# Four modulation rows: columns and a trip through memory in place of full-precision row products

## The reference

```python
mod = (_silu(L0_c) @ L0_wmod).reshape(L0_c.shape[0], 6, 1, -1)
sa, ca, ga, sb, cb, gb = (mod[:, 0], mod[:, 1], mod[:, 2], mod[:, 3], mod[:, 4], mod[:, 5])
ga = (2 * (ga >= 0) - 1) * jnp.maximum(jnp.abs(ga), 0.25)
gb = (2 * (gb >= 0) - 1) * jnp.maximum(jnp.abs(gb), 0.25)
h = _layernorm(x, axis=-1) * (1 + ca) + sa
x = x + ga * _L0_attn_ref(h, L0_attn_Wq, L0_attn_Wk, L0_attn_Wv, L0_attn_Wu, L0_attn_Wo)
h = _layernorm(x, axis=-1) * (1 + cb) + sb
x = x + gb * _L0_ffn_ref(h, L0_ffn_weight, L0_ffn_bias)
```

## Time and profile before

| | |
|---|---|
| median of 3 runs | 508.58 us (508.37 to 510.7) |
| the profiled execution | 510.15 us |
| its span on the slowest core, core 0 | 508.1 us |
| spans of the other cores | 499.9 to 504.5 us |
| TensorE matmuls busy on core 0 | 405.4 us, 80% of the span |
| VectorE busy | 299.4 us, 59% |
| ScalarE busy | 237.8 us, 47% |
| moved by DMA | 84.92 MB, 167 GB/s on average |

### The profile page before, as it was taken

One profiled execution on the slowest core, in us unless ns is written; L12 is line 12 of the kernel. 1 busy time (PEld: TensorE's weight loads), 2 busy tenths in 40 slices (PEclk: granted clock), 3 DMA queues, 4 the chain that ended last, 5 costly groups with the idle time before them and its releaser, 6 DMA issues.

```text
span 508.1 us, 6419 instructions; the slowest of 8 cores (499.9 to 508.1 us)
## 1 busy us (share of the span) xinstructions
PE 405.4 (80%) x2028; PEld 189.4 (37%) x2068; DVE 299.4 (59%) x524; ACT 237.8 (47%) x348; POOL 57.7 (11%) x90
## 2 busy tenths in 40 slices
PE   0004568968989999787796989998999989998984
PEld 0002234424544444433442434443444434444441
DVE  0388550184867627446886456663666637665884
ACT  1134165454457323156756385445764367643431
POOL 1021011020000000000002111111201212011321
PEclk9999996999999999999898899998999989999998
DMA  7999969999956665920229950656335752455686
GB/s 189 336 335 192 268 189 234 215 195 265 304 221 195 248 221 183 306 92 1 83 70 301 318 140 10 124 118 119 54 77 90 159 85 55 111 84 124 88 142 143
DMA packets 17984, 84.92 MB, mean 167 GB/s; under 512 B 2336, under 2 KB 2336, under 8 KB 12832
## 3 DMA queue, kind: packets, MB, share of 16 engines
q0 software_dynamic: 7776, 32.51, 33.8%
q1 hardware_dynamic: 10176, 52.01, 31.4%
HBM read 68.26 MB, written 24.64 MB: 183 GB/s over the span
## 4 chain that ended last, share of the span: by engine, by line
PE 51%; DVE 19%; ACT 12%; issue 11%; DMA 4%; POOL 1%; DVEq 1%; SPq 1%; ACTq 0%; POOLq 0%
PE pb L315 43%; DVE junk L454 4%; DVE bn L266 3%; DMA wa<-wmod_a 3%; ACT rn L619 2%; PE pb L380 2%; ACT osq L609 2%; DVE h L705 2%; DMA stage<-wmod_b 1%; DVE am L708 1%; PE pb L617 1%; PE pb L343 1%; ACT xq L719 1%; DVE wm_c L424 1%; ACT rn L622 1%
## 5 line engine op out<-in xcount | busy, mean ns | idle before, releaser
L315 PE MATMUL pb<-wk_s,h 128*128 128x512 bf16 x249 | 62.0, 405 | 9.1 <-DVE h L463 5.8
L315 PE MATMUL pb<-fq,xqT 128*128 128x512 bf16 x247 | 60.5, 385 | 3.4 <-ACT xqT L731 2.2
L315 PE MATMUL pb<-wo_s,u_s 128*128 128x512 bf16 x254 | 61.2, 394 | 1.5 <-DVE u_s L599 1.4
L315 PE MATMUL pb<-h,wu_s 128*128 128x512 bf16 x248 | 60.5, 385 | 0.3
L315 PE MATMUL pb<-h,wq_s 128*128 128x512 bf16 x250 | 60.2, 384 | 0.2
L315 PE MATMUL pb<-wv_s,h 128*128 128x512 bf16 x249 | 59.3, 386 | 0.4
L285 PE MATMUL pb<-id_b,xh 128*128 128x128 bf16 x128 | 13.3, 260 | 49.5 <-ACT xh L275 47.9
L624 DVE SCALAR_TENSOR_TENSOR q_s<-rn,pb 128x512 bf16<-128x512 f32 x32 | 22.0, 687 | 44.6 <-ACT rn L622 42.1
L315 PEld LDWEIGHTS pb<-wk_s,h 128*128 128x128 bf16 x256 | 25.9, 103 | 43.2 <-issue 18.4
L371 DVE SCALAR_TENSOR_TENSOR accb<-stage,silc,accb 128x1024 f32<-128x1024 f32 x28 | 36.0, 1285 | 8.9 <-DMA stage<-wmod_b 6.5
L315 PEld LDWEIGHTS pb<-wo_s,u_s 128*128 128x128 bf16 x256 | 25.7, 101 | 33.4 <-issue 6.4
(11 more groups left out here) (92 smaller groups left out, 561.1 us busy)
## 6 DMA issues: line engine op xcount, KB each, us to landing
stage<-wmod_b SPq DMA_DIRECT2D x16, 1024.0 KB, 7.0
xr<-x_tm POOLq DMA_DIRECT2D x16, 512.0 KB, 16.6
wa<-wmod_a SPq DMA_DIRECT2D x8, 1024.0 KB, 22.2
xr<-x_tm SPq DMA_DIRECT2D x16, 512.0 KB, 3.6
out_tm<-row_gbb SPq DMA_DIRECT2D x4, 2048.0 KB, 20.1
out_tm<-xr POOLq DMA_DIRECT2D x15, 512.0 KB, 8.1
out_tm<-h POOLq DMA_DIRECT2D x15, 512.0 KB, 5.5
stage<-wo SPq DMA_DIRECT2D x4, 1024.0 KB, 14.0
```

Of the source, the lines that this page charges most:

```text
L315: t = PE.do(lambda e, dc=dc: e.matmul(pb[bank][:], lhs(dc), rhs(dc), start=(dc == 0), stop=(dc == NC - 1)), *after, each(dc) if each else ...
```

## The change

The four vectors `ga`, `sb`, `cb`, `gb` are now made as `sa` and `ca` are: `wmod_b` lies in memory feature by feature, feature 8p+k on partition p, `mod_piece` multiplies it in its stage buffer by `silr` and sums along the row into column `2c+d` of `mod_c[v]`, and `mod_fin` does the sign, maximum and 1+ steps on 128x8 columns. `put` writes the column tile (4 KB, 32 bytes for each partition) to a new tensor `rows` in memory and `get` reads that row back onto all 128 partitions (512 KB), both on the SP queue. The same is done for the bias times `gb` (`put(3)`) and for the weight's scales times `gb` (`put(4)`, in the new `last_row`). The columns `silc` and the products L380 and L815 are gone. For the weight's scales to lie in the same order, the feed-forward weight is loaded with rows 8p+ec, and `ffn_transp` writes every eighth column of `fq`. The list `mods` is in a new order: 4 pieces of vector 0, `mod_fin(0)`; 4 pieces of vector 1, `mod_fin(1)`, the four `wo_piece`; 4 pieces and `mod_fin` of vectors 2 and 3; `get(3)`. The reads `get(0)`, `get(1)`, `get(2)` stand in the SP queue right behind the load of the next vector's first piece. `wa_sum` writes into `wa` itself and no longer into one `junk` tile.

```diff
-                in1=accb[:], op0=ALU.mult, op1=ALU.add), st_tok[n], t_acc[0])
+            st_free[n] = col_tok[v] = DVE.do(lambda e, d=d: e.scalar_tensor_tensor(
+                out=s[:, D * d:D * d + D], in0=s[:, D * d:D * d + D], scalar=1.0, in1=silr[:],
+                op0=ALU.mult, op1=ALU.mult, accum_out=mod_c[v][:, 2 * c + d:2 * c + d + 1]),
+                st_tok[n], t_silr)
+
+    def put(k, col, *after):
+
+        put_tok[k] = SP.dma(sl_p[k], bass.AP(d_rows, k * D, [[NC, 128], [1, NC]]), col[:], *after)
+
+    def get(k, row, *after):
+
+        row_tok[k] = SP.dma(sl_g[k], row[:], bass.AP(d_rows, k * D, [[0, 128], [1, D]]),
+                            put_tok[k], *after)
...
-    def mod_row(v, hf):
-
-        sl = slice(512 * hf, 512 * hf + 512)
-        t = PE.do(lambda e: e.matmul(pb[7][:], on_f[:], accb[:, sl], start=True, stop=True),
-                  t_acc[0], t_ones, b7[0])
...
+    def mod_fin(v):
...
+        col_tok[v] = t
+        put(v, gbb_c if v == 3 else m, t)
...
-            out=fq[:, :, 128 * ec:128 * ec + 128],
+            out=fq[:, :, ec::NC],
...
-        t = None
         for col, k in ((ca_c, 0), (sa_c, 1)):
             t = DVE.do(lambda e, col=col, k=k: e.scalar_tensor_tensor(
-                out=junk[:], in0=wa[dc][:, D * k:D * k + D], scalar=1.0, in1=silr[:],
-                op0=ALU.mult, op1=ALU.mult, accum_out=col[:, dc:dc + 1]), wa_tok[dc], t_silr, t,
-                wa_free.get(dc - 1))
+                out=wa[dc][:, D * k:D * k + D], in0=wa[dc][:, D * k:D * k + D], scalar=1.0, in1=silr[:],
+                op0=ALU.mult, op1=ALU.mult, accum_out=col[:, dc:dc + 1]), wa_tok[dc], t_silr)
...
+    def piece_after(v, k):
+        mod_piece(v, 0)
+        get(k, ROWS[k])
+
+    mods = [lambda c=c: mod_piece(0, c) for c in range(4)]
+    mods.append(lambda: mod_fin(0))
+    for v in (1, 2, 3):
+        mods.append(lambda v=v: piece_after(v, v - 1))
+        mods += [lambda v=v, c=c: mod_piece(v, c) for c in range(1, 4)]
+        mods.append(lambda v=v: mod_fin(v))
+        if v == 1:
+            mods += [lambda c=c: wo_piece(c) for c in range(4)]
+    mods.append(lambda: get(3, row_gbb))
...
     def last_row():
-        t = t_dg[0]
-        for hf in range(2):
...
+
+        t = DVE.do(lambda e: e.tensor_tensor(out=gws_c[:], in0=ws_c[:], in1=mod_c[3][:], op=ALU.mult),
+                   fw_tok[NC - 1], col_tok[3])
+        put(4, gws_c, t)
+        get(4, row_g, fold_tok[0])
...
-    last_rows()
+    last_row()
     fill()
```

More of the change, by code:

```diff
@@ L88, in build_nc @@
     d_wb = dram("wmod_b", [128, 4, NC, D])
+    d_rows = dram("rows", [5, D], kind="Internal")
     d_idb = dram("ident_bf", [128, 128], BF16)
@@ L141, in build_nc @@
     blk = sb("blk", [128, 128], BF16)
-    on_f = sb("on_f", [128, 128])
-    c_col = sb("c_s", [128, NC])
-    silc = sb("silc", [128, NC])
+    bias_c = sb("bias_c", [128, NC])
+    mod_c = [sb(f"mod_c{v}", [128, NC]) for v in range(4)]
+    sgn_c = sb("sgn_c", [128, NC])
+    abs_c = sb("abs_c", [128, NC])
+    gws_c = sb("gws_c", [128, NC])
+    gbb_c = sb("gbb_c", [128, NC])
     sa_c = sb("sa_c", [128, NC])
@@ L197, in build_nc @@
     sl_c = Slot(nc, "const")
-    sl_k = Slot(nc, "const2")
     sl_r = Slot(nc, "crow")
-    sl_b = Slot(nc, "bias")
+    sl_p = [Slot(nc, f"put{k}") for k in range(5)]
+    sl_g = [Slot(nc, f"get{k}") for k in range(5)]
     x_tok = {}
@@ L230, in load_stage @@
         return n
-    t_c = SP.dma(sl_c, c_col[:], d_c.ap())
     t_cr = SP.dma(sl_r, silr[:], bass.AP(d_cr, 0, [[0, 128], [1, D]]))
-    SP.dma(sl_k, id_b[:], d_idb.ap())
-    SP.dma(sl_k, id_h[:], d_idh.ap())
-    t_const = SP.dma(sl_k, blk[:], d_blk.ap())
+    SP.dma(sl_c, id_b[:], d_idb.ap())
+    SP.dma(sl_c, id_h[:], d_idh.ap())
+    SP.dma(sl_c, blk[:], d_blk.ap())
+    t_const = SP.dma(sl_c, bias_c[:], d_fb.ap())
     wa_tok = [SP.dma(sl_a[dc], wa[dc][:],
                      bass.AP(d_wa, dc * 2 * D, [[NC * 2 * D, 128], [1, 2048]])) for dc in range(NC)]
-    t_ones = DVE.do(lambda e: e.memset(on_f[:], 1.0))
     t_half = DVE.do(lambda e: e.memset(halfc, HALF))
@@ L352, in build_nc @@
     b7 = [None]
[L353 to L356, removed]
+    row_tok, col_tok = {}, {}
     fold_tok = [None]
     t_gate = [None]
+    put_tok = {}
     def mod_piece(v, c):
@@ new lines, in mod_fin @@
+    def mod_fin(v):
+        m = mod_c[v]
+        t = col_tok[v]
+        if v == 2:
+            t = DVE.do(lambda e: e.tensor_scalar_add(out=m[:], in0=m[:], scalar1=1.0), t)
+        elif v != 1:
+            t1 = DVE.do(lambda e: e.tensor_scalar(out=sgn_c[:], in0=m[:], scalar1=0.0, scalar2=2.0,
+                                                  op0=ALU.is_ge, op1=ALU.mult), t)
+            t = DVE.do(lambda e: e.scalar_tensor_tensor(out=abs_c[:], in0=sgn_c[:], scalar=1.0, in1=m[:],
+                                                        op0=ALU.subtract, op1=ALU.mult), t1)
+            t = DVE.do(lambda e: e.tensor_scalar_max(out=abs_c[:], in0=abs_c[:], scalar1=0.25), t)
+            t = DVE.do(lambda e: e.scalar_tensor_tensor(out=m[:], in0=sgn_c[:], scalar=1.0, in1=abs_c[:],
+                                                        op0=ALU.subtract, op1=ALU.mult), t)
+        if v == 3:
+            t = DVE.do(lambda e: e.tensor_tensor(out=gbb_c[:], in0=m[:], in1=bias_c[:], op=ALU.mult),
+                       t, t_const)
+        col_tok[v] = t
+        put(v, gbb_c if v == 3 else m, t)
@@ L404, in wo_piece @@
+    ROWS = {0: row_g, 1: row_sb, 2: row_cb, 3: row_gbb}
     def wo_piece(c):
@@ L698, in norm1 @@
             out=h2[g % 4][:], in0=x[:], scalar=mean[:, 0:1], in1=row_cb[:], op0=op, op1=ALU.mult),
-            row_tok[2, 1], y_out.get(g - 4), t, fw_tok[7])
+            row_tok[2], y_out.get(g - 4), t, fw_tok[7])
     def norm2(g):
@@ L856, in build_nc @@
             X[3]()
-        if g == 0:
-            last_row()
     for hf in range(2):
```

75 lines of the change are left out of this document (11 added, 64 removed).

## The result

The changed kernel is slower: 522.25 us (median of 4 executions) against 509.32 for the kernel before on the same chip, ratio 1.0227, 95% interval 1.0164 to 1.029. One of the four executions, at 530.06, ran in a slower state of the chip, with part of its cores at a lower clock; the ratios here leave such executions out, and the other three took 518.51 to 522.44. The forecast of 496.5 and its range to 505 are both missed, on the wrong side.

The account below looks back on a forecast made before the run. PE, its matmuls busy for 80% of the span and half of the chain of waits, was taken as the bound; 510.15 + 2.0 - 11.3 + 1.7 - 5.4 = 497.2, less 0.7, gave 496.5 us, range 489 to 505.

Parts of the forecast that it names:

- The strided `fq`: ACT's write of every eighth column of fq in the weight quantisation: taken as 0, bounded by 0 and +2 us.
- Vector 0, +2.0: Break in SP's loads behind put(0): xhat(12) starts later and PE passes 155.18 two us late; bounds -3.8 and +5.
- Vectors 1 to 3, -11.3: Up to 215.6 us PE waits only for the row products; removing them gains 3.0 + 2.9 + 5.4 us.
- DVE at `kv_bd`, +1.7: DVE ends its list for kv_bd at 208, against PE's arrival at 206.3; bounds 0 and +6 us.
- Weight quantisation, 0: Loads behind put(3) and get(3) land about when the feed-forward weight is read: price 0, bounds 0 to +3 us.
- `last_row`, -5.4: Row of the weight's scales: its PE and DVE work goes, gaining 5.6 us, of which DVE's q takes back 0.2.
- Behind 300 us, 0: Everything behind 300 us was taken as untouched, only shifting along: 0.
- The slower one: Rival, chance 0.07: SP's list stands still in each break, costing 10 us more than reckoned, giving 527 us.
- The doubling rival: Rival, chance 0.17: the strided write of fq doubles in price, adding 2 us to give 498.5.
- my two signs of being wrong: xhat(12) keeping PE's time would mean forecast too high; DVE waiting over 10 us at a put, too low.
- the line "L444 at 1.1 or at 2.2": Listed check on ACT's write of fq: its time in the trace would be 1.1 or 2.2 us.
- The five stretches at the head of the prediction: Time PE loses around the row products: 3.80, 3.00, 2.9, 5.40 and 5.5 us, put together as 20.7.

Follow-up runs that it names:

- the two pairs of kernels: The kernel before with only the strided write added, 535.78 us; the changed kernel with only that write made contiguous, 497.69 us.
- the first probes: The kernel before with three more instructions for each of 19 write or read forms behind its last output; executed once, no kernel time given.
- the first experiment: The changed kernel with fq written in runs of 128 and rows 3 and 4 written as 4-byte elements: 527.09 us, ratio 1.0329 to the kernel before.

## Why the prediction was wrong

**The strided `fq`: the step that failed.** The form of the argument was right. The pace of the stretch hides a slower evacuation up to a point, and what is over it counts. The size was not. I had no row, took 0, and ended the bound at a doubling. The price is 4.3 times: 4805 ns, and 5.88 for a step against a pace of 2.85. Put into my own steps, seven steps are 5.88 - 2.85 = 3.0 longer and the last evacuation 3.7: 24.9. The stretch shows 23.9, the medians of the two pairs of kernels 24.6 and 26.6. But the parts are others, so the closeness of the sum is partly luck. From the start of the first evacuation to the last transposes the kernel before takes 17.65 us (243.84 to 261.49) and the changed one 40.02 (241.23 to 281.25): 22.4. From there to the first result of `wproj` it is 4.23 and 5.81, 1.6 more, at a granted clock of 1.00 and 0.72. The last evacuation, which I had on the path, is not on it. The doubling was no bound from a row, only a factor that felt large. What could have been reckoned was the point from which it decides: the pace of 2.85 less one filling of the bank with its gaps, 0.9, leaves 2.0 us for the evacuation, 1.8 times its 1.113. Beyond that each further microsecond costs seven. With a write that no row showed and a rule of the Trainium skill against it, that belonged into the rivals as the slower case, with more than the 0.07 that I gave to SP's list.

The Trainium skill's rule (SBUF — State Buffer, "Door 1: The DMA port swizzle (why `[64,N]` ≈ `[32,N]`)", two hits in a 16-byte line for full speed) pointed the right way in its part on hits. The same note of the Trainium skill names 8 bf16 as how far one can stride for free; the step of 8 took 4783 here instead of 1113, and the measurement decides. By the two hits the runs of two at 16-byte distance are fast, which L871 agrees with (1207). By them bf16 with step 4, two hits in a line, would be fast as well; L875 of the first probes shows 2522. So the rule on hits fits the 4-byte pieces here and not the single 2-byte ones.

**Vector 0, +2.0.** PE passes its point 1.6 late, `xhat(12)` starts at 141.96 (140.6 reckoned). Right in sum, by two errors that cancel: the break is longer (put 7.1 for 2, load 9.4 for 6.0), and it begins 3.9 earlier, as vector 0's last piece landed at 115.89, not 118.83, and the column steps ended at 119.4, not 122.6. The queue was not drained as I had assumed, with the DMA engines 97% busy over the put; over the eight cores this put takes 4.2 to 7.1. The nearest row for a small write was the wrong one.

**Vectors 1 to 3, -11.3, and DVE at `kv_bd`, +1.7.** PE is through at 205.85 (206.3 reckoned). DVE starts the cast at 211.54 in the profiled execution of after, at 208.69 and 209.87 in the two kernels that differ from it only behind that point; 208 was reckoned. Against PE's 206.3 the term is 2.4 to 5.2, inside its bounds of 0 to +6, above the value taken.

**Weight quantisation, 0.** In after 1.6 are lost, with PE at half clock behind its 4.73 us wait for DVE (that the clock is the whole of it no run shows); with contiguous writes 0.4, and DVE waits 0.90 for the weight's first load. The bounds of 0 to +3 held.

**`last_row`, -5.4.** The stretch from group 0 to group 1 is 5.1 us shorter in after and 4.8 with the contiguous write. Right to within 0.6.

**Behind 300 us, 0.** Wrong by 3 to 4 us in my favour. With the contiguous write three stretches of groups are shorter by 0.9, 1.5 and 0.8, with the same work. The one from 331.74 before and its answer after:

```profile
331.74:350.73 18.99, 16.76 (x78) 7.44 (x78) 10.27 (x16) 11.37 (x17) 3.34 (x4) 0.94 0.57 109
```

```profile
348.34:366.46 18.12, 16.16 (x82) 7.32 (x80) 10.28 (x15) 11.37 (x17) 3.62 (x4) 1.00 0.56 112
```

The granted clock is 0.94 in the one and 1.00 in the other, and likewise 0.91 and 1.00 in the stretch that is 1.5 shorter. I had no step for it. What makes the clock fall there in the kernel before, no run here takes apart. So that the contiguous version came out at 497.69 beside 496.5 is partly luck: it gained 6.0 until `wproj` where 7.6 was reckoned, 4.8 in `last_row`, and 3.5 that I hadn't counted.

**The rivals.** The slower one named SP's list as its mechanism. In the changed kernel that isn't what happened, but the first experiment shows that it was a real danger: with 4-byte elements the same put holds the list 15.8 and 20.7 us and costs 29.4 (527.09 against 497.69; 29.6 by the ratios). The doubling rival had the place and the direction, not the price. Neither of my two signs of being wrong came, either: `xhat(12)` lost its time, and the longest wait of DVE behind a put was 9.83 us, not over 10. Both looked at the breaks, and none at the evacuation; only the line "L444 at 1.1 or at 2.2" would have caught it. (The five stretches at the head of the prediction add up to 20.6, not 20.7; nothing rests on it.)

## What to carry to other kernels

A tile that is written with a step costs by what goes into each 16 bytes, and single 2-byte elements are the dear case; write pairs of neighbours, by turning two pieces into one bank, or put the step on the reading side, where step 8 took 2.1 us instead of 4.8. When an edit has no row, work out from which price it decides before settling on a value, and treat a layout change as an edit to every instruction that touches the tile. A small transfer that holds a queue's list is priced by its elements and by what is queued with it, and belongs behind the loads that others wait for.

## What the runs showed of the hardware

- An ACT write of 1024 bf16 elements at every eighth place takes 4.8 us instead of 1.1, on DVE 2.4 instead of 0.7; in pairs 1.2 and 0.7.
- Reading is cheaper: bf16 with step 8 takes 2.1 us on ACT, with step 4 1.2.
- 4 KB written to memory as 128 pieces of 32 bytes release the next transfer after 1.5 us on a quiet queue and after 4 to 13 beside other loads or the fill; as 1024 pieces of 4 bytes after 8.3 to 33.4 (all cores of all kernels here).
